# A two-layer transformer block: the attention's turn and division moved to 32x32 blocks on VectorE, and the order of all steps written anew

## The reference, cut to what matters

```python
x: (8, 512, 256) float32              # batch, tokens, width; 16 heads of 16
def attention(x, Wqkv, bqkv, Wo, bo):
    q, k, v = heads(split(x @ Wqkv + bqkv))
    scores = einsum('bhid,bhjd->bhij', q, k) * 16 ** -0.5 + alibi_causal_bias
    out = einsum('bhij,bhjd->bhid', softmax(scores), v)
    return out.reshape(8, 512, 256) @ Wo + bo
def ffn(x, W_up, W_gate, W_down):     # 256 -> 1024 -> 256
    wu, wg, wd = ternary_quant(W_up), ternary_quant(W_gate), ternary_quant(W_down)
    return (silu(x @ wu.T) * (x @ wg.T)) @ wd.T
x = layernorm(x + attention(x, ...))
x = layernorm(x + ffn(x, ...))
```

## Time and profile before

| | |
|---|---|
| time of three runs | 621.65 us median (620.36 to 622.35) |
| the profiled execution | span 619.3 us from its first to its last instruction; its device time is not given apart from the three runs', which are 1.1 to 3.1 us above the span |
| PE busy | 583.6 us, 94% |
| DVE busy | 494.4 us, 80% |
| ACT busy | 318.8 us, 51% |
| POOL busy | 299.0 us, 48% |

### The profile page before, as it was taken

The page is one execution under the profiler, slowest core; times in us unless marked ns, Lnnn a source line. Parts: engine busy times, 40 slices in busy tenths (PEclk is TensorE's granted clock), DMA queues, the critical chain, the costliest instruction groups (busy, mean ns, idle before and its releaser), DMA issues.

```text
span 619.3 us, 12888 instructions
## 1 busy us (share of the span) xinstructions
PE 583.6 (94%) x4012; PEld 342.5 (55%) x4012; DVE 494.4 (80%) x1258; ACT 318.8 (51%) x593; POOL 299.0 (48%) x504
## 2 busy tenths in 40 slices
...
GB/s 158 289 175 206 211 51 161 23 29 163 122 172 66 3 229 115 166 1 83 161 166 100 1 199 123 160 28 52 186 144 127 1 166 105 206 2 3 35 1 35
DMA packets 47724, 68.49 MB, mean 111 GB/s; under 512 B 4857, under 2 KB 43641, under 8 KB 44793
## 3 DMA queue, kind: packets, MB, share of 16 engines
...
## 4 chain that ended last, share of the span: by engine, by line
PE 78%; DVE 5%; ACT 5%; POOL 5%; issue 4%; DMA 2%; SPq 0%; POOLq 0%; DVEq 0%
PE ring L698 17%; PE max_bank L613 10%; PE acc L647 9%; PE ring L635 9%; PE ring L590 8%; PE acc L715 7%; PE ring L597 4%; ACT probs L772 4%; PE ring L671 4%; PE max_bank L618 2%; PE ring L655 2%; POOL probs L1042 2%; PE ring L684 1%; POOL tern_down L1085 1%; PE max_bank L715 1%
## 5 line engine op out<-in xcount | busy, mean ns | idle before, releaser
L772 ACT ACTIVATE probs<-ring 128x512 f32<-128x512 f32 x320 | 170.7, 606 | 45.6 <-PE ring L635 44.0
L1042 POOL TENSOR_SCALAR_AFFINE_SELECT probs<-probs 128x256 f32<-128x256 f32 (+1 forms) x320 | 120.5, 401 | 130.1 <-ACT probs L772 129.4
L896 DVE CUSTOM_DVE_ANT_0 max_bank<-max_bank,causal_wide 128x384 f32<-128x384 f32 (+1 forms) x256 | 157.2, 637 | 15.3 <-PE max_bank L613 12.2
L613 PE MATMUL max_bank<-k_stack,q_stack 112*128 112x384 bf16 (+3 forms) x512 | 123.4, 304 | 5.9 <-DVE neg_max L896 2.8
L1078 POOL TENSOR_TENSOR hidden_lo<-hidden,hidden_hi 128x512 f16<-128x512 f32 (+1 forms) x72 | 75.1, 1050 | 63.6 <-ACT hidden_hi L803 63.3
L635 PE MATMUL ring<-q_stack,k_stack 114*128 114x512 bf16 (+3 forms) x512 | 103.7, 300 | 1.6 <-DVE attn L921 0.5
L791 ACT ACTIVATE gating<-ring,tanh_scale 128x512 f32<-128x512 f32 (+1 forms) x72 | 45.8, 639 | 74.0 <-PE ring L698 74.0
L647 PE MATMUL acc<-probs,v_ones 128*32 128x512 f32 (+3 forms) x1024 | 79.9, 437 | 2.8 <-POOL probs L1042 2.8
L613 PEld LDWEIGHTS max_bank<-k_stack,q_stack 112*128 112x128 bf16 x512 | 46.5, 98 | 54.0 <-DVE neg_max L896 15.3
L900 DVE TENSOR_REDUCE neg_max<-max_bank 128x2 f32<-128x512 f32 (+1 forms) x96 | 63.7, 686 | 10.4 <-PE max_bank L618 8.7
L635 PEld LDWEIGHTS ring<-q_stack,k_stack 114*128 114x128 bf16 x512 | 44.5, 97 | 49.4 <-issue 17.0
(11 more groups left out here) (107 smaller groups left out, 866.0 us busy)
## 6 DMA issues: line engine op xcount, KB each, us to landing
...
```

The costliest lines, as they stand in the source:

```text
L613: mm = pe.matmul(max_bank[k][:, width * i:width * (i + 1)], q_stack[0:MAX_ROW, 4 * g + h, P * tile:P * (tile + 1)], k_stack[0:MAX_ROW, 4 * ...
L772: rg.drained(act.activation(probs[:, g % 2, n, :], rg.bank(step)[:, :], ACT.Exp), step)
L896: dve.tensor_tensor_reduce(scores, scores, causal_wide[:, SEQ - width:SEQ], -1.0, LOWEST_START, ALU.add, ALU.min, neg_max[:, g, first_col: ...
L1042: return pool.affine_select(out=v, in_=v, compare_op=ALU.is_ge, fill=0.0, base=0, pattern=([[0, blocks]] if blocks > 1 else []) + [[1, P]] ...
```

## The change

- `nt` and the PE part of `at` are gone. `turn.g` on DVE reads `acc` and writes `pv_t` with every 32x32 block transposed in itself, for all four quads. A head owns 32 partitions, so in `pv_t` each block has tokens on the partitions and one head's 16 values and its sum along the row. `nt_out.g` divides there, now from SBUF, into `mixed`, where quads 2f and 2f+1 share one row of 512. `at.f` transposes the blocks of `mixed[:, f]` back on DVE into `attn_t`. ACT's copies of `acc` and of `attn_t` are gone.
- In `attn_t` the rows now stand in another order, so `load_wo.1` loads the output weights in that order with eight DMAs; `load_wo.0` puts them in plain order into `attn_t`, which is free then, for `bias_fold`.
- `v.u` makes two token tiles at a time in one bank: the same matmuls, half the banks, and two ACT copies of 128x512 instead of four of 128x256.
- All order lists but PRE are written anew. In FIRST the weight loads and `abs_sum` stand first, `ternary.0` and `ternary.2.0` in the middle, and POOL's `load_res` behind the masks.

```diff
-                    elif kind == "nt":
-                        g = step[1]
-                        at_least(pe, acc_drained[g % 2], 3, b, g // 2 + 1 - acc_skipped(name))
-                        for t in range(TT):
-                            mm = pe.transpose(bank[:, P * t:P * (t + 1)], pv_t[:, g % 2, P * t:P * (t + 1)], ident[:, :])
-                        rg.filled(mm, step)
-                    elif kind == "at":
-                        f = step[1]
-                        rg.wait_all_drained(pe, (("nt", 2 + f),), step)
-                        for t in range(TT):
-                            mm = pe.transpose(bank[:, P * t:P * (t + 1)], attn[:, t, P * f:P * (f + 1)], ident[:, :])
-                        rg.filled(mm, step)
...
                         if u == 0:
-                            rg.wait_drained(pe, ("at", f))
-                            pe.wait_ge(weights_in[1], 32)
+                            at_least(pe, attn_turned, FT, b, f + 1)
+                            pe.wait_ge(wo_in, 16 * 4 * FT)
...
-                    elif kind == "pv" and step[1] < 2 and step[2] == TT - 1:
-                        g = step[1]
-                        at_least(act, acc_filled[g % 2], 3, b, g // 2 + 1 - acc_skipped(name))
-                        act.activation(pv_t[:, g % 2, :], acc[g % 2][:, :], ACT.Copy).then_inc(acc_drained[g % 2], 1)
-                    elif kind == "at":
-                        rg.wait_filled(act, step)
-                        rg.drained(act.activation(attn_t[:, step[1], :], rg.bank(step)[:, :], ACT.Copy), step)
...
-                    elif kind == "pv" and step[1] >= 2 and step[2] == TT - 1:
+                    elif kind == "turn":
                         g = step[1]
+                        if not (first and g == 0):
+                            at_least(dve, mixed_done, QUADS, b, g - 1)
                         at_least(dve, acc_filled[g % 2], 3, b, g // 2 + 1 - acc_skipped(name))
-                        dve.tensor_copy(pv_t[:, g % 2, :], acc[g % 2][:, :]).then_inc(acc_drained[g % 2], 1)
+                        dve.transpose(pv_t[:, g % 2, :], acc[g % 2][:, :]).then_inc(acc_drained[g % 2], 1)
...
+                        dve.tensor_tensor(
+                            mixed[:, g // 2, :].rearrange("p (s c) -> p s c", c=32)[:, :, DH * (g % 2):DH * (g % 2 + 1)],
+                            heads[:, :, 0:DH], inv_sum[:, g % 2, :, :].broadcast_to([P, TT * 4, DH]),
+                            ALU.mult).then_inc(mixed_done, 1)
+                    elif kind == "at":
+                        f = step[1]
+                        at_least(dve, mixed_done, QUADS, b, 2 * f + 2)
+                        dve.transpose(attn_t[:, f, :], mixed[:, f, :]).then_inc(attn_turned, 1)
```

More of the change, by code:

```diff
@@ new lines @@
+    take.3.8 exp.2.3 max.3.7 max.3.8 max.3.9 take.3.9 exp.2.4 load_wo.1 take.3.10 exp.2.5 max.3.10 pv.1.1 pv.1.2
+    mt.3 turn.0 mt_out.3 exp.2.6 pv.1.3 turn.1 exp.2.7 part_write.0.0 exp.2.8 qk.1 exp.2.9 exp.3.0 exp.3.1 exp.3.2
+    nt_out.0 exp.3.3 pv.2.0 nt_out.1 exp.3.4 pv.2.1 exp.3.5 pv.2.2 qk_out.1 split.0 split.1 exp.3.6 exp.3.7 exp.3.8
+    at.0 pv.2.3 part_write.1.0 exp.3.9 part_write.1.1 pv.3.0 load_res ternary.2.1 turn.2 pv.3.1 pv.3.2 pv.3.3
+    part_write.0.1 ternary.1 nt_out.2 turn.3 nt_out.3 part_write.0.2 wo.0.0 part_write.1.2 wo.1.0 at.1 ternary.2.2
@@ L142 @@
+    wo.0.1 stack_read.0 wo.1.1
 """
 SECOND_ORDER = """
[L145 to L148 removed]
@@ L164 @@
-    at.0 nt.3 wo.0.0 nt_out.3 at.1 stack_read.0 store wo.1.0 wo.0.1 wo.1.1
+    max.0.0 load_next take.0.0 take.0.1 max.0.1 qk.2 v.0 max.0.2 take.0.2 max.0.3 part_write.2.0 take.0.3 take.0.4
+    max.0.4 take.0.5 take.0.6 take.0.7 v_out.0 max.0.5 ln1 take.0.8 max.0.6 x1_lo.0 max.0.7 take.0.9 x1_lo.1 v.1
+    max.0.8 take.0.10 take.1.0 part_write.2.1 take.1.1 max.0.9 split.2 swish.0 part_write.2.2 v_out.1 swish.1 x1t.0
+    x1t.1 qk.3 mt_out.0 max.0.10 split.3 max.1.0 up.0 max.1.1 up.1 swiglu.0 mt.0 take.1.2 swish.2 part_write.3.0
@@ new lines @@
+    pv.0.3 exp.1.8 exp.1.9 exp.2.0 part_write.0.2 take.3.6 max.3.9 exp.2.1 ffn_sum.0 exp.2.2 ffn_sum.1 take.3.7
+    take.3.8 max.3.10 split.0 ffn_stats.0 qk.1 exp.2.3 take.3.9 mt.3 exp.2.4 pv.1.0 exp.2.5 take.3.10 qk_out.1
+    exp.2.6 mt_out.3 split.1 exp.2.7 exp.2.8 pv.1.1 exp.2.9 turn.0 pv.1.2 ffn_stats.1 pv.1.3 part_write.1.0 turn.1
+    exp.3.0 exp.3.1 exp.3.2 exp.3.3 nt_out.0 ln2 exp.3.4 pv.2.0 exp.3.5 exp.3.6 exp.3.7 nt_out.1 pv.2.1 exp.3.8
+    exp.3.9 store pv.2.2 at.0 pv.2.3 part_write.1.1 turn.2 pv.3.0 pv.3.1 part_write.1.2 pv.3.2 nt_out.2 pv.3.3
@@ L165 @@
+    turn.3 nt_out.3 wo.0.0 at.1 stack_read.0 wo.1.0 wo.0.1 wo.1.1
 """
 LOOP_ORDER = """
-    qk.2 max.0.0 max.0.1 take.0.0 qk.3 take.0.1 v.0 max.0.2 ln1 x1t.0 max.0.3 x1t.1 max.0.4 v.1 v_out.0 take.0.2
-    load_res take.0.3 max.0.5 v.2 part_write.3.0 max.0.6 max.0.7 x1_lo.0 take.0.4 take.0.5 part_write.2.0 x1_lo.1
-    v_out.1 v_out.2 split.2 up.0 take.0.6 take.0.7 gate.0 swish.0 max.0.8 up.1 swiglu.0 split.3 take.0.8
-    part_write.2.1 max.0.9 up.2 take.0.9 hidden_hi.0 up.3 max.0.10 swish.1 gate.1 max.1.0 swish.2 take.0.10 gate.2
@@ L205 @@
[L205 to L209 removed]
+    qk.2 part_write.3.0 part_write.2.0 take.0.0 part_write.2.1 max.0.0 max.0.1 qk.3 take.0.1 ln1 part_write.2.2
@@ L223 @@
+    hidden_hi.5.1 swiglu.5.1 hidden_hi.6.1 hidden_hi.7.1 swish.7.1 gate.7.1 down.1.1 swiglu.6.1 swiglu.7.1 down.2.1
+    down.3.1 ffn_sum.0 down.4.1 down.5.1 ffn_stats.0 ffn_sum.1 ffn_stats.1 ln2.0 down.6.1 down.7.1 ln2.1
 """
```

206 lines of the change are left out of this document (99 added, 107 removed).

## The result

| | before | changed | ratio, 95% interval |
|---|---|---|---|
| median | 622.0 us (4 runs) | 668.2 us (667.0 to 673.4, 4 runs) | 1.076 (1.070 to 1.081) |
| span of the profiled execution | 619.3 | 665.2 (its time 667.0) | |

The change makes the kernel slower by 7.6%, where 598 us were forecast. The page of the changed kernel, against the earlier trace rows: us, share of the span, instructions.

The account below looks back on a forecast made before the run. PE was taken to set the pace throughout, with DVE also full in an iteration's first stretch. 619.3 - 21.1 (transposes) - 2 (start) - 1 (end) = 595.2 us of span, plus 2.35 to the median: 597.5, say 598; range 590 to 611.

Parts of the forecast that it names:

- The price of the turns: On DVE: each 128x512 transpose costs 0.69 us, like the copy it replaces; 2.76 us more an iteration.
- rival E: On DVE: a float32 block transpose takes 1.4 us, twice the copy, making the kernel slower, 631 us; chance 0.09.
- PE's relief: On PE: 192 transposes leave, 48 groups at 0.44 us, gaining 21.1 us, or 2.64 an iteration.
- I book no change of waits: 0: In the stretch after pv.0: waits among the turns, products and output projection stay as they were, 0 us.
- has 7.8 us to spare in the second: DVE in the iteration's last 23.90 us, after pv.0: busy 16.13 us, 67%, so room for the turns.
- rival B: In the loop: DVE's queue takes back half the gain, 1.3 us an iteration, 608 us; chance 0.17.
- The sign that the prediction gave for B: Cheap turns but a long loop, 69.3 us an iteration, with the waits on L613 for DVE saying where.
- The start: In FIRST: less POOL work behind the last mask, later second stack read; between 5 us gained and 7 lost, 2 gained taken.
- Rival C: In FIRST: second stack read lands 14 us later, DVE idles 10, the start loses 7, 607 us; chance 0.10.
- Blocking: DVE instructions with two SBUF inputs and POOL exclude each other; booked 0, at most 1.7 us if all four blocked once.
- The end: In LAST: the first half's sum and statistics fill DVE's 1.90 us wait for the last down; 1 us gained.

Follow-up runs that it names:

- old_orders: The changed kernel's code with the order lists of the kernel before, turns in place of nt; 639.2 us, ratio 1.027.
- The pads: Two runs: the kernel before plus four idle DVE transposes per loop iteration, ahead of split.1 (628.9 us) or behind it (621.3 us).
- old_split: old_orders with, in the loop, DVE's splits ahead of the turns and SP's part writes and first stack read ahead of the store; 642.1 us, ratio 1.036.
- read_ahead: The changed kernel with stack_read.1 directly behind part_write.3.2 in SECOND, LOOP and SEVENTH; 651.8 us, ratio 1.047.
- split_ahead2: read_ahead with, in the loop, DVE's splits ahead of turn.0 and ln2, and SP's part writes and stack_read.0 ahead of the store; 640.0 us, ratio 1.031.
- first_reads: read_ahead with FIRST changed: second stack read and mt_out.0 ahead of the weight loads, ACT's sums of magnitudes among the exponentials; 658.0 us, ratio 1.059.
- hybrid: The kernel before with only quads 2 and 3 turned on DVE; 630.7 us, ratio 1.016.

## Why the prediction was wrong

**The price of the turns was right.** 0.71 us against 0.69 taken; rival E, by which they would cost 1.4, is refuted, though it was the only one that said slower. The estimate of 0.71, worked out from the figure that the Trainium skill gives in "VectorE: DVE Perf Modes", section "The three transpose paths", agrees with the trace's 0.712.

**PE's relief was right as a count, wrong as a gain.** 192 matmuls left. In the best order that kept all turns on DVE, old_orders, an iteration takes 70.9 us and not 68.0: all of the 2.64 came back as waits (3.7 us of them against 0.8). DVE's work came out as forecast there, 62.3 us against 62.2.

**The step that failed is "I book no change of waits: 0", and behind it the sentence that DVE "has 7.8 us to spare in the second".** The 67% of that stretch is a mean over two parts. Up to `split.1`, which ends at 295.0, DVE waits 0.3 us at a time at most, and behind it it waits for links of its own chain (`pv`, `nt`, `wo`) in five gaps of 6.1 us together. The pads showed the price of 2.8 us of work in the first part, 1.6 us, and in the second, 0. The turns can't all stand in the second: old_split put them there, and PE waited for `pv_t`, `x` and `attn_t` instead. This was rival B in kind, but it took half where it was all. The sign that the prediction gave for B fails in the changed kernel itself: its waits for DVE's maxima are 6.6 us in all against 5.4, and those for the stack read 39.1 against none.

**The larger loss was in no step.** The prediction followed PE and DVE and, of SP's queue, only the start. In the loop the new lists put `stack_read.1` behind `mt_out.0`, where the old ones had it ahead (3.1 us an iteration, read_ahead). And they left the splits behind `ln2` and the part writes behind the store, as the old ones did, while the end of the iteration behind them got shorter, so that the first read was issued 2.9 us ahead of `z` and not 6.8 (from the last split to `z` 6.9 us and not 8.9, from that split to the read's issue 4.0 and not 2.1); with it issued 9.2 ahead, an iteration took 3.2 us less (split_ahead2, which goes beyond the old order). Together this makes up for 6.3 of the 7.8 us that an iteration grew, the low clock behind the waits included: the granted clock of the loop is 0.96, 0.95 and 1.00 in the changed kernel, read_ahead and split_ahead2. What remains, 72.1 against 68.0, is not taken apart by a run. DVE's added work is in it, as in old_orders, and so is blocking by POOL, for the normalisations of `x` took 3.01 us in split_ahead2 and PE waited 1.9 us an iteration for `x`. DVE's busy time of 64.2 us there, where 62.2 were forecast, holds the 1.6 by which they are longer. The prediction named no row of the reads in the loop, though before one was issued at 297.13 for a use at 306.24, 9.1 us for a landing of 7.8 (the median on the page): a margin of 1.3 us.

**The start.** Forecast 2 us shorter, it is 11.2 longer. Rival C's signs came true: the second read was issued at 41.68 and not 31.68, the first `max` of quad 2 came at 51.75 (50 or later was its sign), and PE waited 8.2 us for `max_parts`, whose hand-over stands behind that read in SP's queue. The power for `ln1` came at 100.68, where near 92 was forecast. Blocking, which the prediction booked at nothing, cost some 11.5 us in old_orders, but POOL's long steps stand elsewhere in the changed kernel: DVE's four ternary steps took their short times, and one product 1.26 us for 0.42. There it was POOL that was held up: in the chain that ended last a mask of about 0.4 us took 2.55 beside DVE's ternary step of 2.35, and PE waited 4.9 us for the masks. How much of the 11.2 us each of the two waits is worth no run says, since first_reads was spoiled. The reading of the earlier trace rows had this in it unseen: the 7.47 us of POOL's first step, which began beside such a step of DVE, were 5.4 to 5.6 in the changed kernel, old_orders and hybrid.

**The end** came as forecast: 0.7 us shorter for 1 taken.
